# PE's window addresses in bytes and ahead of their tiles, and expansion's one-hots moved from VectorE to ScalarE

## The reference

```python
xl, xr = x @ Wl.T + bl, x @ Wr.T + br                  # rows per node
m = xl[src] + xr[dst] + edge_attr @ We.T               # layers a and b; c, d, e have other scores
score = where(m > 0, m, 0.2 * m) @ att
es = exp(score - segment_max(score, dst)[dst])         # softmax over the edges of one destination
alpha = es / segment_sum(es, dst)[dst]
out = segment_sum(alpha[:, None] * xl[src], dst)       # and then norm, residual and so on
```

## Time and profile before

| | |
|---|---|
| time, median of 3 runs | 13585.27 us (13582.88 to 13586.3) |
| the profiled execution | 13576.47 us, span 13574.4 us |
| the five streams, from the first gather to the last | 11085 us of the span |
| PE busy | 77% |
| PE weight load | 64% |
| DVE busy | 63% |
| ACT busy | 18% |
| POOL busy | 68% |

### The profile page before, as it was taken

How to read it: one execution, slowest core, us unless ns; L and a number is a source line. 1 busy time by engine, 2 the same in 40 slices (tenths; PEclk the granted TensorE clock), 3 DMA queues, 4 the chain that set the end, 5 groups by cost and what they waited for, 6 DMA issues and landing times. The chain is left out here.

```text
span 13574.4 us, 346433 instructions
## 1 busy us (share of the span) xinstructions
PE 10504.2 (77%) x102671; PEld 8732.6 (64%) x102672; DVE 8519.3 (63%) x15786; ACT 2406.7 (18%) x4954; POOL 9220.1 (68%) x8386
## 2 busy tenths in 40 slices
PE   2388888857888888488888857888888578888872
PEld 1377777746777777377777735777777357777762
DVE  7567777755777777355555544777777446666664
ACT  0011212111111122022222211111111112222220
POOL 0177777756777776577777735777777257777761
PEclk9855556555555555555555555555555555555555
DMA  0333333323333332222222223232222233333320
GB/s 16 84 75 71 73 73 73 73 42 75 72 72 73 73 71 57 39 55 54 55 54 55 54 54 106 77 78 77 77 78 72 69 96 78 78 78 78 78 64 11
DMA packets 771899, 912.63 MB, mean 67 GB/s; under 512 B 400125, under 2 KB 447616, under 8 KB 769760
## 3 DMA queue, kind: packets, MB, share of 16 engines
q0 software_dynamic: 267232, 390.16, 15.0%
q1 hardware_dynamic: 503008, 498.92, 13.0%
HBM read 791.99 MB, written 96.35 MB: 65 GB/s over the span
## 5 line engine op out<-in xcount | busy, mean ns | idle before, releaser
L914 POOL DMA_INDIRECT bs_gat<-table_b,bs_idx x1568 | 1750.7, 1117 | 506.5 <-issue 477.5
L914 POOL DMA_INDIRECT ds_gat<-table_d,ds_idx x1568 | 1749.3, 1116 | 506.7 <-issue 506.7
L914 POOL DMA_INDIRECT as_gat<-table_a,as_idx x1568 | 1740.9, 1110 | 506.6 <-issue 477.5
L914 POOL DMA_INDIRECT es_gat<-table_e,es_idx x1568 | 1725.7, 1101 | 505.6 <-issue 505.6
L914 POOL DMA_INDIRECT cs_gat<-table_c,cs_idx x1568 | 1731.0, 1104 | 491.0 <-issue 491.0
L1174 PE MATMUL ds_psM<-dstW_d,ds_hot 128*128 x9408 | 1252.7, 232 | 194.4 <-DVEq L1107 72.2
L1174 PE MATMUL es_psM<-dstW_e,es_hot 128*128 x9408 | 1253.5, 226 | 175.9 <-issue 65.3
L1174 PE MATMUL cs_psM<-dstW_c,cs_hot 128*128 x9408 | 1232.0, 183 | 182.3 <-DVEq L1100 68.9
L1174 PEld LDWEIGHTS ds_psM<-dstW_d,ds_hot 128*128 128x128 bf16 x9408 | 972.2, 103 | 481.6 <-issue 241.1
L1174 PEld LDWEIGHTS es_psM<-dstW_e,es_hot 128*128 128x128 bf16 x9408 | 962.6, 102 | 480.8 <-issue 224.4
L1174 PEld LDWEIGHTS cs_psM<-dstW_c,cs_hot 128*128 128x128 bf16 x9408 | 967.5, 103 | 473.0 <-issue 223.3
(11 more groups left out here) (758 smaller groups left out, 17937.2 us busy)
## 6 DMA issues: line engine op xcount, KB each, us to landing
as_rank<-rel_d SPq DMA_DIRECT2D x196, 256.0 KB
as_ea<-in_eaT SPq DMA_DIRECT2D x196, 256.0 KB
bs_rank<-rel_d SPq DMA_DIRECT2D x196, 256.0 KB
bs_ea<-in_eaT SPq DMA_DIRECT2D x196, 256.0 KB
cs_rank<-rel_d SPq DMA_DIRECT2D x196, 256.0 KB, 3.2
ds_rank<-rel_d SPq DMA_DIRECT2D x196, 256.0 KB, 3.3
es_rank<-rel_d SPq DMA_DIRECT2D x196, 256.0 KB, 3.4
table_e<-et_st SPq DMA_DIRECT2D x49, 544.0 KB, 2.7
```

The lines of the kernel that those rows point to most:

```text
L914: g_.indirect_dma_start(gat[s][:, j, :], None, table, bass.IndirectOffsetOnAxis(ap=idxS[s][:, j:j + 1].bitcast(U32), axis=0)).then_inc(got ...
```

## The change

It has two parts.

Part one, PE's addresses. Before, each matmul of `expand` forms its address from w as a slice counted in elements, when the matmul is written. Now `dst_rows` forms the six addresses of a tile in bytes (w times the row's bytes, plus a constant) for two tiles together, and for the pair after the one that is multiplied next. `sum_rows` does the same in `collect`, for the four tiles of a half ahead of that half's wait and matmuls. The matmuls are the same ones in the same order.

Part two, the one-hots. DVE's `onehot` goes. ACT makes `hot` in four operations: for each of the two windows a square of (rank - partition number) into a new tile `off`, and a relu of 1 minus that, which is 1 where they are equal and 0 elsewhere. It stands at the end of ACT's step u, for group u+2, and it waits on `fed`, `made` of g-2, its own last relu (`hots`), and for each relu on its square (`apart`). In DVE's step it stood right after the flush.

```diff
-                iota(m["pid"][:, :], pattern=[[P, 2]], base=0, channel_multiplier=1, ...)
+                memset(m["one"][:, :], 1.0)
+                iota(m["pidN"][:, :], pattern=[[-P, 2]], base=0, channel_multiplier=-1, ...)
...
 # ScalarE
+                def onehot(it, s):
+                    g = it * RING + s
+                    a.wait_ge(fed[s % 4], it * (3 * FEED) + (s // 4) * FEED + FEED)
+                    wait(a, made, g - 1)
+                    wait(a, hots, g)
+                    for x in range(2):
+                        a.activation(off[:, x, :], rank[s % 4][:, :], ACT.Square, bias=m["pidN"][:, x:x + 1]).then_inc(apart, 1)
+                    for x in range(2):
+                        a.wait_ge(apart, g * 2 + (x + 1))
+                        last = a.activation(hot[s % 2][:, x, :], off[:, x, :], ACT.Relu, bias=m["one"][:, 0:1], scale=-1.0)
+                    last.then_inc(hots, 1)
...
+                    if within(u + 2, GROUPS):          # at the end of step
+                        onehot(...)
...
 # VectorE
-                def onehot(it, s):
-                    g = it * RING + s
-                    v.wait_ge(fed[s % 4], it * (3 * FEED) + (s // 4) * FEED + FEED)
-                    wait(v, made, g - 1)
-                    for a in range(2):
-                        last = v.tensor_scalar(hot[s % 2][:, a, :], rank[s % 4][:, :], m["pid"][:, a:a + 1], None, ALU.is_equal)
-                    last.then_inc(hots, 1)
...
 # TensorE
+                def dst_rows(some):
+                    at = [[[dstB[:, bass.ds(w * (2 * dc) + (part * WINS + a) * (2 * dc), 2 * dc)].bitcast(BF16) for part in range(3)]
+                           for a in range(2)] for w in some]
+                    for one in at:
+                        for a in range(2):
+                            for part in range(3):
+                                pe.lower_ap(one[a][part])
+                    return at
+                def sum_rows(h, w):
+                    at = [sumB[h][:, bass.ds(w * (4 * CW) + a * (4 * CW), 4 * CW)].bitcast(F32) for a in range(2)]
+                    for a in range(2):
+                        pe.lower_ap(at[a])
+                    return at
...
+                    at = dst_rows(windows[0:2])
                     for j in range(GROUP):
-                        w = windows[j]
+                        if j % 2 == 0 and j + 2 < GROUP:
+                            at += dst_rows(windows[j + 2:j + 4])
...
-                                last = pe.matmul(o, hot[s % 2][:, a, j * P:(j + 1) * P], dstAt[a][part][:, bass.ds(w, 1), :],
+                                last = pe.matmul(o, hot[s % 2][:, a, j * P:(j + 1) * P], at[j][a][part],
...
                     for h in range(2):
+                        at = [sum_rows(h, windows[FL * h + j]) for j in range(FL)]
                         pe.wait_ge(zeroed, k * 2 + (h + 1))
```

More of the change, by code:

```diff
@@ L18 @@
 BF16 = mybir.dt.bfloat16
+U8 = mybir.dt.uint8
 I32 = mybir.dt.int32
@@ L155, in build @@
             rankX=sb("rankX", [P, 2 * P, GROUP], BF16),
-            pid=sb("pid", [P, 2]),
+            pidN=sb("pidN", [P, 2]), one=sb("one", [P, 1]),
             vec=sb("vec", [P, len(VECS), D]),
@@ L265, in prepare @@
         LOADS = 10
-        MADE = 22
+        MADE = 23
         with nc.Block() as block:
@@ L328, in _ @@
                        allow_small_or_imprecise_dtypes=True).then_inc(made, 1)
-                g.iota(m["pid"][:, :], pattern=[[P, 2]], base=0, channel_multiplier=1,
+                g.memset(m["one"][:, :], 1.0).then_inc(made, 1)
+                g.iota(m["pidN"][:, :], pattern=[[-P, 2]], base=0, channel_multiplier=-1,
                        allow_small_or_imprecise_dtypes=True).then_inc(made, 1)
@@ L811, in stream @@
         hot = [sb(f"hot{s}", [P, 2, GE], BF16) for s in range(2)]
+        off = sb("off", [P, 2, GE], BF16)
         ahot = [sb(f"ahot{s}", [P, 2 * P, GROUP], BF16) for s in range(2)]
@@ L848, in stream @@
         masked = [sem(f"masked{s}") for s in range(3)]
-        hots, made, took, scored, sch, xch, ready, blank, wl, pch, sub, past = (
-            sem(n) for n in ("hots", "made", "took", "scored", "sch", "xch", "ready", "blank", "wl", "pch", "sub", "past"))
+        hots, made, took, scored, sch, xch, ready, blank, wl, pch, sub, past, apart = (
+            sem(n) for n in ("hots", "made", "took", "scored", "sch", "xch", "ready", "blank", "wl", "pch", "sub", "past", "apart"))
         turned, ended, gaveE, carried, gaveC, lowered, exped, backed, alphad = (
@@ L944, in step @@
                         a.activation(alpha[xs][:, 0, :], psY[:, 384:384 + CT], ACT.Copy).then_inc(alphad, 1)
+                    if within(u + 2, GROUPS):
+                        if known(u):
+                            onehot((u + 2) // RING, (u + 2) % RING)
+                        else:
+                            onehot(it if s + 2 < RING else it + 1, (s + 2) % RING)
+                onehot(0, 0)
+                onehot(0, 1)
                 rounds(a, step, END)
@@ L1118, in step @@
                         flush(k - 2, (ks - 2) % RING)
[L1119 to L1123, removed]
                     if within(k - 1, GROUPS):
@@ L1147, in step @@
                         score(it, s)
-                onehot(0, 0)
-                onehot(0, 1)
                 rounds(v, step, END)
@@ L1153, in _ @@
             def _(pe):
[L1154 to L1157, removed]
+                dstB = dstW[:, :, :, :].rearrange("p t w f -> p (t w f)").bitcast(U8)
+                sumB = [psA[h][:, :].bitcast(U8) for h in range(2)]
+                def dst_rows(some):
[11 more added lines that the diff above has]
+                    return at
                 def expand(it, s):
@@ L1183, in collect @@
                     for h in range(2):
+                        at = [sum_rows(h, windows[FL * h + j]) for j in range(FL)]
                         pe.wait_ge(zeroed, k * 2 + (h + 1))
                         for j in range(FL * h, FL * h + FL):
-                            w = windows[j]
                             for a in range(2):
                                 for part in range(3):
-                                    last = pe.matmul(sums[h][a][:, bass.ds(w, 1), :], ahot[ks % 2][:, a * P:(a + 1) * P, j],
+                                    last = pe.matmul(at[j - FL * h][a], ahot[ks % 2][:, a * P:(a + 1) * P, j],
                                                      parts[ks % 3][:, part, j, :], start=False, stop=False, skip_group_check=True)
```

## The result

The kernel before takes 13,584 us (median of 4 runs beside those of the changed one), the changed kernel 13,416 us (13,412 to 13,422). The ratio is 0.988, with a 95% interval of 0.987 to 0.989. In a second series on one chip it was 13,419 against 13,603 us, 0.987 (0.985 to 0.988). The forecast was 13,425 us.

What follows compares the result with a forecast made beforehand. POOL's back-to-back gathers were taken to bound the streams. From 13,576.5 us, minus 160 for one-hots, plus 0 for ACT and 0 for PE, gave 13,416; the median lies 9 higher, so 13,425 us. 80% range: 13,290 to 13,595.

Steps and rivals of the forecast that it cites:

- POOL paces the streams: In the five streams, POOL issues gathers back to back and never waits for DVE; streams are 82% of the span.
- The hold, DVE's end plus 0.81 us: A gather begun during certain DVE operations ends 0.81 us after that operation; all such waits cost 1,279 us.
- What the one-hots are worth, 160 us: Taking the one-hots off DVE shortens the held gathers by 160 us, 0.16 us a group.
- the first steps' row: Layer a's first steps, DVE doing only one-hots and scores: gathers take 0.969 us, 180 us over 980 groups if one-hots alone.
- the bounds of 0 and 350 us: Gain from one-hots leaving DVE: 0 if gathers meet the next operation, 350 us if the longest waits need the whole run.
- shares of DVE's time: One-hots' 185.5 us of 1,100 us of holding DVE operations in layer b, 17% of 1,279 us: 217 us.
- whole runs break up: Rival: long gathers need the unbroken run of DVE work, so 350 us go, 13,235 us; chance 0.08.
- ScalarE's operations, 1.06 us: Each of ACT's four new 1,024-column operations takes 1.06 us, 4.2 us a group, hidden, so 0 in the sum.
- `expand`, 4.5 us for its 48 matmuls: On PE, the 48 matmuls fall from 6.35 to 4.5 us, bounds 3.1 and 6.35; 0 in the sum.
- PE stands for `hot`: PE waits 1.9 us in the chunk step, once in four groups: 0.5 us a group, up to 1.4 in layer d.
- The rival on the other side: Rival: PE's loop becomes the pace if addresses cost as before, 290 us more, 13,875 us; chance 0.12.
- gathers meet the next operation: Rival: gathers let through earlier are held by DVE's following operation instead, time the same, 13,585 us within 20; chance 0.12.

## Why the prediction was right

- **POOL paces the streams: right.** Three comparisons have the change in time beside that of the gathers' busy time: -167 us of gathers and -168 us of time for the change, -589 and -592 without the comparison, -466 and -439 with it in PSUM. The last pair is apart by 27 us. Of these, 19 lie between and behind the streams (the stretches from one stream's last gather to the next one's first, and from the last gather to the end, are that much longer in sum): a longer DVE step is paid after the last gather. The other 8 are the difference between the profiled execution and the median.
- **The hold, DVE's end plus 0.81 us: right,** seen again after (0.82), and shown by the unused comparisons, by the comparison moved to PSUM with layer d as control, and by the count in the table.
- **What the one-hots are worth, 160 us: 167 measured, and the size was luck.** The figure came from the first steps' row, taken as the one in which one-hots stand almost alone. They have no part in it. Six of its 40 gathers are above 0.96 us; five of them end 0.81 to 0.82 us after the end of one of the score's operations, L1095 or L1096, and the sixth (0.974) was not held by one. In the changed kernel, without one-hots on DVE, the same stretch has a mean of 0.973 us where it was 0.969. Nor does the sum name what the one-hots did to the operations behind them: they themselves let go of gathers held for 90 us, and the gain was 167. Its sign was argued soundly, and the bounds of 0 and 350 us were wide. The other way of working it out, by shares of DVE's time, is not a law either. It gives 217 us for the one-hots, which gave 167. By the same share L1086 would give 238.5 / 1,100 x 1,279 = 277 us, and taking it away gave 589. The range given for that run (185 to 365 us less) was built on such shares and missed. What one operation costs depends on what stands before and after it in the step. That is the mechanism of the rival "whole runs break up", which had a chance of 0.08: it had a part in this change (L1127), and it is most of what the comparison's removal gave.
- **ScalarE's operations, 1.06 us: a term too small.** They take 1.133 us, four 4.25 us in the timeline instead of 4.2, since two of a kind overlap a little (2.17 for two). The rows of 512 and 544 columns that I extended are copies without a bias from a tile, and the new operations have one; no run here separates what that costs from what the columns cost. The formula of the Trainium skill (ScalarE: Activation LUTs, "What ACT_TABLE_LOAD costs") for an operation with such a bias gives 280 + 0.833 x 1,024 = 1,133 ns, and the rows agree. It stayed without effect, as the kernel with 1,934 us more on ScalarE shows.
- **`expand`, 4.5 us for its 48 matmuls: 1.65 in layer c**, below my lower bound of 3.1. The bound came from `collect`, whose matmuls write 68 columns; those of `expand` in layer c cost 34 ns each once no address stands between them. In layer b the 4.9 us are of the whole expansion, f32 matmuls (0.78 us for two) included, and must be set beside the 6.6 us before: 1.7 us less, where 1.9 were forecast. So PE's cycle in layer b came out nearly as forecast, and in layer c far shorter.
- **PE stands for `hot`: right in kind, too small.** I had 0.5 us a group. It is 529.2 us in layer b, 2.7 a group. A faster PE asks earlier, and what it gains in `expand` it mostly stands for. This is the loop's slack, and hence no time.
- **The rival on the other side** was right about its mechanism: with part one missing, the loop is late and 13,815 - 13,594 = 221 us are lost against before, where 290 were priced. It didn't come about because the addresses did become cheap. The rival "gathers meet the next operation" did not come about in the sum, but it is why the copies out of PSUM still cost about 60 us: by the count above they held nothing, and gathers met other operations.

## What to carry to other kernels

When GpSimd issues indirect DMAs back to back, price a VectorE operation by whether it holds them, and by the run of holding operations it stands in, not by its time: an operation nearly twice as long with one operand in PSUM was worth 3.3% of this kernel. Before moving work off an engine, work out the round trip that the other engine's lateness closes. Here one half of the change alone was worth nothing and the other alone cost 1.7%, and only together did they win. An engine's busy time that falls by a quarter of the span tells nothing until the engine that paces has been named. And ask of the row that gives a price which operation made it long; here the price was read from gathers that a different operation had held.

## What was not expected of the hardware

- A VectorE comparison of 128x2048 with one operand in PSUM (2,278 ns) let all 1,078 gathers that began inside it, counted as in the table, finish in 0.94 to 0.96 us. The same comparison with both operands in SBUF (1,217 ns) held every one, to 1.42 us at least.
- For the stream's large operations it is all or nothing; a few small scans lie between (L1002: 0.95 to 1.07 us). In the kernel before, reductions of a 128x512 f32 tile in SBUF (L1097, L1104, L1111) held none of the 446 gathers that began inside them, and the score's two operations just before the first of them (L1095, L1096), of the same size and place, held all 290.
- The same kernel took 13,594 and 13,603 us on two chips and 18,416 us on a third. The trace kept there is of a variant of the changed kernel: its matmuls are as long as elsewhere, and PE is idle in "issue" between them. The cause stays open. A ratio is worth only what the chip under it has as its pace.
- Register work for addresses shows as PE busy time: 48 matmuls went from 6.35 to 1.65 us in layer c with the same matmuls in the same order, and not by a faster clock (granted over the stream: 0.54 in both).
